# Layer 1's experts: the second output part over all 128 rows, gates and diagonals made among the shared experts, and a third shared output in a bank of its own

## What is computed

```python
logits = xf @ gate_w + gate_b
scores = jax.nn.softmax(logits, axis=-1)
top_vals, top_idx = jax.lax.top_k(scores, 2)
cw = (one_hot(top_idx, 16) * top_vals[..., None]).sum(axis=1)
h = einsum('td,edh->teh', xf, w1) + b1        # hidden width 176
g = einsum('td,edh->teh', xf, w3) + b3
y = einsum('teh,ehd,te->td', silu(h) * g, w2, cw) + cw @ b2
z = silu(xf @ sw1 + sb1) * (xf @ sw3 + sb3) @ sw2 + sb2   # shared, hidden width 352
return y + z                                   # times gb, added to x
```

## Time and profile before

| | us |
|---|---|
| median of 3 runs | 486.87 |
| lowest and highest run | 486.09, 489.3 |
| the profiled execution, its own time | 486.82 |
| its span (first to last instruction) | 485.1 |
| PE busy in the span | 418.7 (86%) |
| DVE, ACT, POOL busy | 362.5, 291.2, 254.7 |
| mean granted clock of PE, share of full | 0.946 |

### The profile page before, as it was taken

How to read it: one execution, slowest core, us unless ns; L and a number is a source line. 1 busy time by engine, 2 the same in 40 slices (tenths; PEclk the granted TensorE clock), 3 DMA queues, 4 the chain that set the end, 5 groups by cost and what they waited for, 6 DMA issues and landing times.

```text
span 485.1 us, 11398 instructions
## 1 busy us (share of the span) xinstructions
PE 418.7 (86%) x2670; PEld 323.6 (67%) x2670; DVE 362.5 (75%) x1189; ACT 291.2 (60%) x753; POOL 254.7 (53%) x340
## 2 busy tenths in 40 slices
PE   2979953199999996878999999999897979999995
PEld 2657752199999995345655665566555558888885
DVE  5859986046666666899999999999945537777764
ACT  2447641045555553668888888887555247777771
POOL 4013757125545556334556677666566019776662
PEclk9999965579999998899999999999898999999999
DMA  8901226778888751432113140000001321332226
GB/s 242 284 19 42 75 59 157 131 205 256 259 234 256 200 163 52 100 77 66 45 24 77 39 95 19 5 25 13 11 23 45 101 59 37 85 99 77 63 82 204
DMA packets 60802, 49.79 MB, mean 103 GB/s; under 512 B 18124, under 2 KB 49933, under 8 KB 60738
## 3 DMA queue, kind: packets, MB, share of 16 engines
q1 hardware_dynamic: 52338, 36.96, 29.6%
q0 software_dynamic: 5056, 8.48, 5.3%
q10 hardware_dynamic: 3344, 3.62, 2.8%
HBM read 37.25 MB, written 13.73 MB: 105 GB/s over the span
## 4 chain that ended last, share of the span: by engine, by line
PE 54%; DVE 26%; issue 9%; ACT 3%; POOL 3%; DMA 3%; SPq 1%; DVEq 0%; ACTq 0%; POOLq 0%
PE bank L1848 9%; PE bank L1827 9%; PE bank L1882 5%; PE bank L2008 4%; PE bank L1819 3%; DVE qk_sums L1441 3%; PE bank L1941 3%; DVE sums L1464 3%; POOL sorted_tokens L841 3%; PE bank L1981 3%; DVE big L1434 2%; DVE work L1478 2%; PE bank L1836 2%; PE bank L2006 2%; PE bank L1838 2%
## 5 line engine op out<-in xcount | busy, mean ns | idle before, releaser
L856 POOL DMA_INDIRECT results<-work x94 | 92.8, 988 | 78.6 <-DVE work L1389 56.1
L1882 PE MATMUL bank<-late,work 128*128 128x512 f32 x192 | 93.5, 616 | 2.6 <-ACT work L1031 2.4
L998 ACT ACTIVATE work<-bank,mcol 128x128 f32<-128x128 f32 x94 | 43.0, 458 | 43.6 <-PE bank L1819 43.1
L1882 PEld LDWEIGHTS bank<-late,work 128*128 128x128 f32 x192 | 34.1, 197 | 33.2 <-issue 29.7
L1827 PE MATMUL bank<-work,big 128*128 128x128 f32 x376 | 51.5, 281 | 0.0
L1848 PE MATMUL bank<-big,work 128*128 x376 | 50.5, 278 | 0.1
L1827 PEld LDWEIGHTS bank<-work,big 128*128 128x128 f32 x376 | 47.4, 198 | 0.0
L1848 PEld LDWEIGHTS bank<-big,work 128*128 128x128 f32 x376 | 46.6, 195 | 0.3 <-issue 0.3
L1375 DVE TENSOR_SCALAR work<-bank,b_columns 128x128 f32<-128x128 f32 x94 | 28.6, 346 | 24.1 <-PE bank L1827 24.1
L1007 ACT ACTIVATE work<-bank,b_columns 128x128 f32<-128x128 f32 x94 | 29.7, 364 | 27.4 <-PE bank L1827 27.3
L841 POOL DMA_INDIRECT sorted_tokens<-late,router_at x32 | 31.2, 976 | 20.2 <-issue 8.2
(11 more groups left out here) (264 smaller groups left out, 1080.5 us busy)
## 6 DMA issues: line engine op xcount, KB each, us to landing
big<-in_W SPq DMA_DIRECT2D x47, 256.0 KB, 3.3
work<-sorted_tokens SPq DMA_DIRECT2D x94, 65.0 KB, 2.0
big<-results SPq DMA_DIRECT2D x14, 256.0 KB, 3.1
big<-in_w SPq DMA_DIRECT2D x48, 56.0 KB
sorted_tokens<-zeros SPq DMA_DIRECT2D x26, 65.0 KB, 2.1
big<-in_w SPq DMA_DIRECT2D x48, 32.0 KB
results<-work POOLq DMA_INDIRECT x94, 2.9
xres<-in_x SPq DMA_DIRECT2D x4, 256.0 KB, 5.5
```

The source lines that it names most:

```text
L856: pool.indirect_dma_start(ys[l], bass.IndirectOffsetOnAxis(xg[b][:, D:D + 1].bitcast(I32), 0), yo[b], None, bounds_check=TOPK * T - 1, oob ...
L998: act.activation(xgT[b % 2], bank[:, ends[b % 2], 0:P], ACT.Identity, bias=scale_shift[0], scale=scale_shift[1]).then_inc(e_xTc, 1)
L1882: last = pe.matmul(bank[:, 2 * k + i, :], h3T[b], Wqkvb[:, k * HD + i * 512:k * HD + (i + 1) * 512], start=True, stop=True)
```

## The change

1. The second output part multiplies all 128 rows instead of 64. The lower 64 rows of its weights are cleared by DVE in step 0 of layer 1's attention (16 x 128 columns), the lower 64 rows of its activations by POOL (two tiles of 128x128).
2. `gate_differences` and the rest of the softmax (now `gate_shares`) move from behind the shared experts to between the gates of group 0 and the additions; ACT's exponential moves between its silus of groups 1 and 2.
3. POOL no longer waits for the four additions before it makes ones and diagonals, and the diagonals lie in `late`, the projection weights of the attention, which are free by then.
4. The third group's shared output goes to bank 7, so that the fourth, in bank 6, waits for the second group's addition only. PE turns slot 0 between these two outputs.
5. DVE copies the weights of slots 0 and 1 ahead of the last two additions. PE waits for the additions of groups 2 and 3 one and two slots later, where their banks are written again.

```diff
-        diagonals = [[big[:, ob + 2 * NT * D + P * (TOPK * h + k):ob + 2 * NT * D + P * (TOPK * h + k + 1)]
-                      for k in range(TOPK)] for h in range(NT // 2)]
+        diagonals = [[late[:, P * (TOPK * h + k):P * (TOPK * h + k + 1)] for k in range(TOPK)] for h in range(NT // 2)]
...
+        shared_bank = (6, 6, 7, 6)
...
-            pool.wait_ge(router1["gated"], 5)
-            pool.wait_ge(f_x, T // 512)
+            pool.wait_ge(d_vT, 2 * NT)
+            pool.wait_ge(d_sum, DS * NT)
             pool.wait_ge(f_one, 2)
             for b in range(2):
+                pool.memset(hbT[b][:, P:2 * P], 0.0).then_inc(f_one, 1)
+            pool.wait_ge(f_one, 4)
+            for b in range(2):
                 pool.memset(hbT[b][P - 32:P, 0:P], 1.0).then_inc(f_one, 1)
-            pool.wait_ge(f_one, 4)
+            pool.wait_ge(f_one, 6)
+            pool.wait_ge(router1["gated"], 5)
+            pool.wait_ge(d_v, NT)
...
-            for t in range(T // 512):
-                shared_silu(t)
+            shared_silu(0)
+            shared_silu(1)
             act.preload_act_table_set("natural_log_exp_and_others")
             act.wait_ge(router1["gated"], 2)
             act.activation(router1["ex"][:, :], router1["dx"][:, :], ACT.Exp).then_inc(router1["exps"], 1)
             act.preload_act_table_set("silu_and_others")
+            shared_silu(2)
+            shared_silu(3)
...
             def layer1_constants(t, b, q):
 
+                if t == 0:
+                    dve.memset(w2s[HC:P, :].rearrange("p (e c d) -> p e c d", e=E, c=2)[:, :, 1, :], 0.0)
...
+            def fetch_weights(t, e):
+                after(dve, e_h, SLOTS + 2 * (t - NF + 1) if t >= NF else 0)
+                dve.tensor_copy(w13r[:, t % NF, :], w13s[:, bass.ds(e * 2 * H1, 2 * H1)]).then_inc(e_hb, 1)
...
             for part in places[0:3]:
                 part(15, 3, 3)
+            gate_differences()
             for c in range(len(SC)):
                 shared_gate(1, c)
+            gate_shares()
             tiles_of_experts(1)
             shared_add(0)
...
             for c in range(len(SC)):
                 shared_gate(3, c)
+            dve.wait_ge(ld_w1, W1_LOADS)
+            for t in range(AHEAD):
+                fetch_weights(t, experts(t, 1)[0])
             shared_add(2)
-            gate_differences()
             shared_add(3)
...
-                after(pe, f_x, t)
+                after(pe, f_x, 2 if t == 3 else min(t, 2))
...
-                    o = bank[:, 6, i * D:(i + 1) * D]
+                    o = bank[:, shared_bank[t], i * D:(i + 1) * D]
...
             shared_out(2)
+            pe.wait_ge(f_a, len(SC) * T // 512 + 1)
+            slot_turn(1)(0, 0, 0, None)
             shared_out(3)
-            pe.wait_ge(f_x, T // 512)
             pe.wait_ge(t_ready, 2)
...
+                if t == 1:
+                    pe.wait_ge(f_x, T // 512)
                 pe.wait_ge(e_act, 2 * (t + 1))
...
-                pe.matmul(bank[:, 5 + b % 2, 0:D], hbT[b % 2][0:HC, P:2 * P],
-                          w2s[0:HC, bass.ds(e * 2 * D + D, D)], start=False, stop=True).then_inc(e_o, 1)
+                pe.matmul(bank[:, 5 + b % 2, 0:D], hbT[b % 2][:, P:2 * P],
+                          w2s[:, bass.ds(e * 2 * D + D, D)], start=False, stop=True).then_inc(e_o, 1)
```

More of the change, by code:

```diff
@@ L1532, in shared_add @@
                 xi = xres[:, t * 512:(t + 1) * 512]
-                dve.tensor_tensor(xi, xi, bank[:, 6, :], ALU.add).then_inc(f_x, 1)
+                dve.tensor_tensor(xi, xi, bank[:, shared_bank[t], :], ALU.add).then_inc(f_x, 1)
             lg1 = router1["lg"][:, :, :, :].rearrange("p g i e -> p (g i) e")
@@ L1544, in gate_differences, with gate_shares @@
                                   ).then_inc(router1["gated"], 1)
+            ex1 = router1["ex"][:, 0:NT * E].rearrange("p (t e) -> p t e", e=E)
+            top_ex = router1["ex"][:, NT * E:NT * (E + TOPK)].rearrange("p (t k) -> p t k", k=TOPK)
+            def gate_shares():
+                dve.wait_ge(router1["exps"], 1)
+                dve.reduce_sum(router1["se"][:, 0, :], ex1, AX_X).then_inc(router1["gated"], 1)
+                dve.wait_ge(router1["gated"], 3)
+                dve.reciprocal(router1["se"][:, 1, :], router1["se"][:, 0, :]).then_inc(router1["gated"], 1)
+                dve.wait_ge(router1["gated"], 4)
+                dve.tensor_tensor(gates[:, :, :], top_ex, router1["se"][:, 1, :].unsqueeze(2).to_broadcast([P, NT, TOPK]),
+                                  ALU.mult).then_inc(router1["gated"], 1)
+            AHEAD = 2
+            def fetch_weights(t, e):
+                after(dve, e_h, SLOTS + 2 * (t - NF + 1) if t >= NF else 0)
+                dve.tensor_copy(w13r[:, t % NF, :], w13s[:, bass.ds(e * 2 * H1, 2 * H1)]).then_inc(e_hb, 1)
             moments5(14, 2, 3)
@@ L1610, in gated_parts, with later_weights @@
                                          ALU.add, ALU.mult).then_inc(e_act, 1)
-            def fetch_weights(t, b, q, e):
-                after(dve, e_h, SLOTS + 2 * (t - NF + 1) if t >= NF else 0)
-                dve.tensor_copy(w13r[:, t % NF, :], w13s[:, bass.ds(e * 2 * H1, 2 * H1)]).then_inc(e_hb, 1)
-            dve.wait_ge(f_one, 4)
-            dve.wait_ge(ld_w1, W1_LOADS)
-            run_slots(dve, SLOTS, NX, [(0, None), (0, fetch_weights), (4, scaled_result1), (2, gated_parts)], experts)
+            def later_weights(t, b, q, e):
+                if t >= AHEAD:
+                    fetch_weights(t, e)
+            dve.wait_ge(f_one, 6)
+            run_slots(dve, SLOTS, NX, [(0, None), (0, later_weights), (4, scaled_result1), (2, gated_parts)], experts)
             def add_result(t, k):
@@ L1997, in _, with later_turn @@
             shared_out(2)
+            pe.wait_ge(f_a, len(SC) * T // 512 + 1)
+            slot_turn(1)(0, 0, 0, None)
             shared_out(3)
-            pe.wait_ge(f_x, T // 512)
             pe.wait_ge(t_ready, 2)
+            def later_turn(t, b, q, e):
+                if t == 1:
+                    pe.wait_ge(f_x, T // 512 - 1)
+                if t:
+                    slot_turn(1)(t, b, q, e)
             def slot_out1(t, b, q, e):
+                if t == 1:
+                    pe.wait_ge(f_x, T // 512)
                 pe.wait_ge(e_act, 2 * (t + 1))
@@ L2007, in slot_out1 @@
                           w2s[0:HA + 1, bass.ds(e * 2 * D, D)], start=True, stop=False)
-                pe.matmul(bank[:, 5 + b % 2, 0:D], hbT[b % 2][0:HC, P:2 * P],
-                          w2s[0:HC, bass.ds(e * 2 * D + D, D)], start=False, stop=True).then_inc(e_o, 1)
+                pe.matmul(bank[:, 5 + b % 2, 0:D], hbT[b % 2][:, P:2 * P],
+                          w2s[:, bass.ds(e * 2 * D + D, D)], start=False, stop=True).then_inc(e_o, 1)
             pe.wait_ge(ld_w1, W1_LOADS)
-            run_slots(pe, SLOTS, NX, [(0, None), (0, slot_turn(1)), (1, slot_hidden1), (3, slot_out1)], experts)
-            pe.wait_ge(f_one, 4 + NT)
+            run_slots(pe, SLOTS, NX, [(0, None), (0, later_turn), (1, slot_hidden1), (3, slot_out1)], experts)
+            pe.wait_ge(f_one, 6 + NT)
             pe.wait_ge(e_yo, 2 * SLOTS)
```

10 lines of the change are left out of this document (removed).

## The result

The changed kernel takes **476.8 us** (median of 5 executions, 472.2 to 477.8) against 487.8 for the kernel before in the same series: a ratio of 0.9755, 95% interval 0.9716 to 0.9795. The prediction was 472.4, range 469.0 to 479.5: the direction and the range hold, the point is 4.4 us too low.

A forecast was written before the change was run, and what follows sets the result against it. The prediction took PE to bound layer 1's expert loop, with POOL the slowest after the change. Span 485.1 - 16.0 (end) + 1.6 (zeros) = 470.7, plus 1.7 from span to execution, gave 472.4 us; range 469.0 to 479.5.

The forecast's parts named there:

- 128 rows, 0.34 a slot: Layer 1's expert loop: widening the second output part cuts PE's slot from 1.56 to 1.22 us, 15.0 over some 44 slots.
- Rival A: Expert loop: only part of the excess goes, or DVE or ACT bounds; slot 1.40, time 477.4 us; chance 0.07.
- POOL becomes the pace: Layer 1's expert loop: POOL, with a scatter every 1.302 us, becomes slowest and decides when results can be read back.
- The junction, 3.9: End of the shared experts: the first hidden part starts at 396.3 instead of 400.24, 3.9 us earlier.
- The cover: Junction: moved work hides behind waits, such as DVE's for shared outputs; without it the slots would be late by that work.
- The zeros: Step 0 of layer 1's attention: DVE's clearing takes 2.29 us and delays the first tile, costing 1.6 of the span.
- The end: Program's end: data decide, and the last closing pair starts at 463.7 instead of 479.70, 16.0 us earlier.
- path of reads and closing pairs: After the loop: first read at 455.0, all data there 8.5 later at 463.5, last closing pair at 463.7.
- what follows is as before: After the last closing pair: the rest stays unchanged, so its 16.0 us go fully into the span.
- scatters of slots without tokens: End of POOL's loop: six scatters follow slot 40's, and the first read of results does not wait on them.
- the 2.13: End of the loop: the first read follows slot 40's scatter by 2.13 us, so it comes at 455.0.
- The sum: Whole program: span 485.1 - 16.0 + 1.6 = 470.7, plus 1.7 gives 472.4 us; chance 0.83.

The follow-up runs named there:

- e1: Kernel before plus only the 128-row second output part and its zeros; junction and diagonals as they were: 484.6 us, ratio 0.9906.
- e2: Changed kernel with the second output part over 64 rows again and without the zeros: 483.6 us, ratio 0.9920.
- e4: Changed kernel with the second output part over 65 rows (one row of zeros) instead of 128: 477.0 us, ratio 0.9755.
- e9: Changed kernel in which POOL again waits for all four additions of the shared experts before making the diagonals: 481.7 us, ratio 0.9876.
- first profile: First profiled execution of the changed kernel, nothing altered, the fastest of its five: 472.22 us, span 470.5.
- after_again: Changed kernel measured once more in a second series, nothing altered: 477.5 us, ratio 0.9782.
- e10: Changed kernel plus 18 unread unit-matrix products on PE ahead of the first turn of layer 1's attention: 476.9 us, ratio 0.9742.
- e5: Changed kernel with SP waiting for ring buffers 8 to 15 before 0 to 7 ahead of reading results back: 476.4 us, ratio 0.9785.
- e6: Changed kernel plus 17 unread unit-matrix products on PE between the loop and the closing pairs: 478.1 us, ratio 0.9814.
- e15: e11 with POOL's scatters for the empty slots 40 to 46 of layer 1 left out: 470.7 us, ratio 0.9650.
- e7: Changed kernel with DVE clearing the zeros among the shared experts, ahead of the second addition: 472.4 us, ratio 0.9680.
- e11: Changed kernel with the changes of e7 and e5 together: 473.9 us, ratio 0.9677.

## Why the prediction was right, and where it failed

**128 rows, 0.34 a slot: right.** e1, e2 and e4 show it from three sides, and the limit is sharper than claimed. Rival A is out with a mean slot of 1.226, though DVE had even less to spare than written: L1614's row lasts 0.34 and not 0.30, which makes 1.20 against 1.22.

**POOL becomes the pace: right**, at 1.293 against 1.302 (e9). The pause behind the second scatter, 1.39 more than the usual 0.30, was missing in the sum. It stands in the kernels whose first scatter comes about 10 us after C (1.69 or 1.70, in e2 2.16) and not in the kernel before, e1 or e9; its cause is open.

**The junction, 3.9: right** (3.92 in the chain, 4.0 in e2). The cover that the prediction named holds.

**The zeros: the mechanism right, the term mis-sized.** The step "I put the loss at 1.6 of the whole span" counted the delay of the first tile and got it to 0.02. It took PE's pace behind that as given. The loss is 3.5 on average, in the first profile since more of the next tiles' work runs at half clock; in after_again it is 2.7 (164.1 - 161.4), in part open (e10). The question what a longer wait does to PE's clock was not asked, though the profile of before had stretches at half clock at the same place. The price of the clearing itself was well bounded: 2.24 with its late start, against 2.29 taken from a sum over as many columns. The Trainium skill, VectorE: DVE Perf Modes, Zero memsets can be issued as uint32 (trn2), has one cycle an element, about 2.1 us as an estimate; the row has less, 1.76, and with the late start a little more, 2.24.

**The end: the failed step.** The prediction let the program end by the path of reads and closing pairs, "what follows is as before", and set aside the scatters of slots without tokens, "on which it does not wait". SP's reads don't wait for them, but the program's end does: POOL's drain. C to the end fell by 14.2 to 14.5, as POOL's last scatter did, not by 16.0. From the prediction's own numbers it would have been: first scatter 400.8, 46 more at 1.302 makes 460.7, the missing pause 1.4, and 9.0 to the end (from the rows of before: 485.1 - 476.1) makes 471.1; the zeros at 3.5 bring it to 474.6, the span of after_again. (That the two agree so closely is chance: after_again lost less by the zeros and more in layer 0.) The path of the data was mis-sized as well: counted from C, the last pair starts 13.0 earlier than before and not 16.0. Against the prediction the first read is 1.3 late, about the pause of POOL; the last read lands 9.2 and not 8.5 behind the first one's issue; and the last pair starts 1.2 and not 0.2 behind that landing. SP was done 79.2 after C, so without the drain, too, the end would not have come 16.0 ahead of the 94.5 of before. Also, the 2.13 between "slot 40's scatter" and the first read was no such distance: slots count from 0, the last real one is 39, and the read follows it by the landing, 2.20, and by SP's eight waits that remain, about 1.5. The two mistakes, the wrong slot and the wrong distance, cancelled: 400.8 + 39 x 1.302 + 3.67 makes 455.3, where the prediction had 455.0.

**The sum.** For after_again: forecast span 470.7, seen 474.6. The zeros 2.7 instead of 1.6 make 1.1; C to the end 14.2 instead of 16.0 makes 1.8; layer 0 took 0.9 longer in this execution than in the one the sum started from, which the change does not touch; 0.1 is left. In the first profile, the same errors were met by 2.8 from B to C and 0.8 in layer 0 to its favour. The other executions of the changed kernel have no traces; their times, 475.9 to 479.6, lie 0.4 below to 3.3 above the second profile's 476.3, all at a lower granted clock (0.928 to 0.939 against 0.942). That the median, 476.8, lies beside rival A's 477.4 is chance: A's slot of 1.40 did not occur. The range holds the median because its upper part was left for A.

## What to carry to other kernels

Look at the program's last barrier before you say what ends it: an engine that is long done with useful work can hold the end by its queue's drain, and then nothing gained on the path of the data counts (e5, e6), while leaving out seven empty transfers does (e15). When a wait is lengthened in front of PE, price the clock behind it too, or put the work where an engine waits anyway (e7). Two parts of a change that each meet another engine's pace can be worth 6.4 and 4.0 alone and 14.3 together, so test them alone before you credit either.

## What was not expected of the hardware

- POOL's drain at the end lasts until 8.2 (e15) or 8.7 to 9.0 us (all others) after the start of its last scatter, though slot 39's scatter lands after 2.2, and that of slot 46 after 4.0 to 4.7 where its landing is on record (before, after_again, e1, e4, e6, e11).
- For this piece the limit between slow and fast is exactly between 64 and 65 rows (0.41 and 0.22), with the cost also on the piece behind (0.26 and 0.11 for the turn).
- Clearing 64 x 2048 numbers on DVE takes 1.76 us, and so does clearing 1 x 2048 (e4); it starts 0.48 late at the first step of the attention and among the shared experts (e7), beside different work of POOL.
- The stretches at half clock move from execution to execution: from B to C they go with times from 35.4 us (granted clock 1.00) to 39.5 us (0.91), for nearly the same work.
